# Waits by halves in a feed-forward phase; output moved into the next turn and a pipeline without work past its end in a recurrent phase

## The reference

```
ot = einsum('bhd,bhde->bhe', qt, S) + D * sum(qt * kt) * vt
kS = einsum('bhd,bhde->bhe', kt, S)
S  = at * (S - bt * kt[..., :, None] * kS[..., None, :]) + bt * kt[..., :, None] * vt[..., None, :]
```

## Time and profile before

| | |
|---|---|
| median of 3 runs | 4524.77 us |
| the profiled execution | 4536.98 us |
| its span, first to last instruction | 4535.2 us |
| PE busy | 4091.2 us (90%) |
| DVE busy | 3013.7 us (66%) |
| ACT busy | 1967.2 us (43%) |
| POOL busy | 1644.9 us (36%) |
| instructions | 93208 |

### The profile page before, as it was taken

The page is one execution under the profiler, slowest core; times in us unless marked ns, Lnnn a source line. Parts: engine busy times, 40 slices in busy tenths (PEclk is TensorE's granted clock), DMA queues, the critical chain, the costliest instruction groups (busy, mean ns, idle before and its releaser), DMA issues.

```text
span 4535.2 us, 93208 instructions
## 1 busy us (share of the span) xinstructions
PE 4091.2 (90%) x32914; PEld 2709.2 (60%) x32914; DVE 3013.7 (66%) x6409; ACT 1967.2 (43%) x4156; POOL 1644.9 (36%) x1479
## 2 busy tenths in 40 slices
PE   5999999999999999579999999989999999989998
PEld 4545555555555555347666767767676677667666
DVE  3555555555555555487777867867677678778677
ACT  2444444444444443244534435444445445444454
POOL 2111111111111111145454645555464556456454
PEclk9999999999999999798898998998998989989999
DMA  2000000000000000111111111111111111111111
GB/s 99 1 15 1 15 1 15 1 15 1 15 1 15 1 15 1 62 30 32 28 32 24 31 33 31 24 45 19 31 38 21 40 24 31 34 31 24 45 19 35
DMA packets 316505, 110.49 MB, mean 24 GB/s; under 512 B 290096, under 2 KB 303664, under 8 KB 315184
## 3 DMA queue, kind: packets, MB, share of 16 engines
q1 hardware_dynamic: 315968, 103.69, 9.7%
HBM read 77.45 MB, written 26.74 MB: 23 GB/s over the span
## 4 chain that ended last, share of the span: by engine, by line
PE 35%; DVE 11%; issue 5%; ACT 4%; POOL 1%; DMA 1%; SPq 1%; DVEq 0%; POOLq 0%; ACTq 0%
PE d_ps L1780 6%; DVE d_acc L1465 4%; PE d_ps L1856 3%; PE d_ps L1979 3%; PE d_ps L1964 3%; PE d_ps L1999 3%; PE d_ps L1818 2%; PE d_ps L1758 2%; PE d_ps L1893 1%; PE d_ps L1835 1%; PE d_ps L1907 1%; PE d_ps L1827 1%; DVE d_pw L1568 1%; PE d_ps L1797 1%; DVE d_AT L1514 1%
## 5 line engine op out<-in xcount | busy, mean ns | idle before, releaser
L229 POOL TENSOR_TENSOR f_qk<-f_m 128x512 f32<-128x512 f32 x128 | 162.8, 1272 | 1463.7 <-DVE f_m L412 1463.7
L1465 DVE SCALAR_TENSOR_TENSOR d_acc<-d_ps,d_cw,d_acc 128x511 f32<-128x511 f32 (+2 forms) x630 | 468.3, 744 | 81.8 <-ACT d_acc L1248 65.9
L1780 PE MATMUL d_ps<-d_xnT,d_wqkv 128*128 128x512 f32 x840 | 478.6, 700 | 0.2 <-DVE d_acc L1465 0.2
L312 ACT ACTIVATE f_pr<-f_sm,f_nb,f_qsc 128x256 f32<-128x256 f32 (+1 forms) x512 | 289.1, 566 | 160.9 <-DVE f_nb L440 159.1
L689 PE MATMUL f_ps<-f_m,f_w 128*128 128x512 f32 (+1 forms) x768 | 338.5, 595 | 22.6 <-DVE f_m L484 22.6
L1248 ACT ACTIVATE d_acc<-d_ps,d_cw 128x512 f32<-128x512 f32 x210 | 162.4, 774 | 396.6 <-PE d_ps L1780 394.7
L1126 POOL TENSOR_TENSOR d_rn<-d_ss,d_mhalf 128x8 f32<-128x8 f32 x137 | 236.5, 1726 | 253.2 <-DVE d_ss L1486 250.6
L434 DVE CUSTOM_DVE_ANT_0 f_sm<-f_ps,f_mask 128x256 f32<-128x256 f32 (+1 forms) x512 | 179.2, 387 | 210.4 <-PE f_ps L604 207.2
L1121 POOL TENSOR_TENSOR d_qk<-d_m 128x512 f32<-128x512 f32 x138 | 174.8, 1266 | 380.2 <-DVE d_m L1476 372.6
L1283 ACT ACTIVATE d_m<-d_qk 128x512 f32<-128x512 f32 x138 | 86.7, 628 | 421.3 <-POOL d_qk L1121 421.3
L689 PEld LDWEIGHTS f_ps<-f_m,f_w 128*128 128x128 f32 (+1 forms) x768 | 134.4, 178 | 222.9 <-issue 187.1
(11 more groups left out here) (210 smaller groups left out, 9694.0 us busy)
## 6 DMA issues: line engine op xcount, KB each, us to landing
d_wqkv<-in_dwqkv SPq DMA_DIRECT2D x36, 768.0 KB, 4.6
blocks_scratch<-d_LT SPq DMA_DIRECT2D x136, 64.0 KB, 2.0
d_T<-inverse_scratch SPq DMA_DIRECT2D x136, 64.0 KB, 2.2
f_xin<-in_x SPq DMA_DIRECT2D x9, 512.0 KB, 4.1
d_xnT<-xnT_scratch SPq DMA_DIRECT2D x9, 512.0 KB, 5.3
d_xnG<-xnT_scratch SPq DMA_DIRECT2D x9, 512.0 KB, 6.6
d_LB<-blocks_scratch SPq DMA_DIRECT2D x68, 64.0 KB, 2.8
inverse_scratch<-d_TB SPq DMA_DIRECT2D x68, 64.0 KB, 5.0
```

The lines of the kernel that those rows point to most:

```text
L312: nc.scalar.activation(pr[:, u % AHEAD, j, k0:], sm[:, u % AHEAD, j, k0:], ACT.Exp, bias=nb[:, u % AHEAD, j:j + 1], scale=qsc[:, 0, w, h:h ...
L1465: V.scalar_tensor_tensor(out=a[:, k:], in0=ps[:, CV_BANK[n], 0:T - k], scalar=cw[:, X, s * CT + t, TAPS - 1 - k:TAPS - k], in1=a[:, k:], o ...
L1780: last = mm(ps[:, CV_BANK[n], :], wqkv[:, X, k, t * P:(t + 1) * P], xnT[:, k, :], start=k == 0, stop=k == KC - 1)
```

## The change

The first phase: three of the eight copies of q/k transposes (`DVE_TURN = (3, 5, 7)`) go to DVE under a semaphore of their own; the output projection is made for the first three windows (384 tokens) ahead of the last window's transpose and copy, and then for the last 128 tokens; the q/k projections and the up projection wait for each half of their input where they use it.

The second phase: `group(b, k)` says which group a stage works on and returns nothing outside 0 to 31; each stage is left out where there is none. The prologue is the same code at steps -3 to 0, the loop runs 7 times over 4 steps, and the last three turns and the last output stand behind it. `output` of batch b is called in the tail of the first turn of batch b+1: product 0 behind convolution 0, product 1 behind convolution 1, transposes behind convolution 3, into banks 0 and 1. z is its own gate tile, the squares of the output heads go to the tile of the rotation (m12) and no more to oT. L1911 is gone: DVE transposes the 32-row blocks of Rf into T64.

```diff
+DVE_TURN = (3, 5, 7)
...
+                def copy_qkT(n):
+                    part, w = TURN[n]
+                    dve.wait_ge(qkT_ps, 1 + it * 2 * NT + n + 1)
+                    nc.vector.tensor_copy((qT, kT)[part][:, :, w * P:(w + 1) * P],
+                                          ps[:, 4 + n % 2, :].rearrange("p (a t) -> p a t", a=PAIRS)).then_inc(qkT_dve, 1)
+
                 sum_squares(2 * NT - 1)
                 inverse_norm(0)
+                copy_qkT(DVE_TURN[0])
...
+                for n in DVE_TURN[1:]:
+                    copy_qkT(n)
...
                     for c in range(KC):
+                        if n == 0 and l == 0:
+                            pe.wait_ge(xT_rdy, 1 + b * KC + c + 1)
+                        elif n == 0:
+                            pe.wait_ge(x2_rdy, 1 + it * KC - KC + c + 1)
...
+                split = (NT - 1) * P
+                pe.wait_ge(oT_rdy, 1 + it * NT + NT - 1)
+                pe.wait_ge(sm_rdy, 1 + it * NT * FH + NT * FH)
+                project_o(0, 0, split)
                 transpose_o(NT - 1)
+                project_o(1, 0, split)
                 pe.wait_ge(oT_rdy, 1 + it * NT + NT)
                 for c in range(KC):
+                    project_o(c, split, T).then_inc(wo_ps, 1)
...
-                pe.wait_ge(xc_rdy, 1 + it * KC + KC)
...
+                            if m == 0 and part == 0:
+                                pe.wait_ge(xc_rdy, 1 + it * KC + c + 1)
...
+    def group(b, k):
+
+        if isinstance(b, int) and not 0 <= b * NG + k < B * NG:
+            return None
+        return b * NG + k, k % NG, b + k // NG
...
         def merge32_end(i):
-            dve.wait_ge(t32_ps, 1 + i + 1)
-            V.tensor_scalar(T64[32:64, :, 0:32], ps[32:64, 0, :].rearrange("p (q t) -> p q t", q=NQ), -1.0, None,
-                            ALU.mult).then_inc(t64_rdy, 1)
+            dve.wait_ge(rf_b, 1 + 2 * i + 1)
+            V.transpose(T64[32:64, :, 0:32], Rf[0:32, :, 32:64]).then_inc(t64_rdy, 1)
...
+            if put is not None:
+                pe.wait_ge(xo_rdy, 1 + put * 2 + 2)
...
-            q2 = slice(32, 64)
-            for m in range(NQ):
-                last = mm(ps[q2, 0, 32 * m:32 * m + 32], R32[q2, m, :], Y32[q2, m, :], start=True, stop=True)
-            last.then_inc(t32_ps, 1)
...
+        for step in range(-3, 1):
+            turn(0, step)
+        with pe.Fori(0, B - 1) as b:
+            for step in range(1, NG + 1):
+                turn(b, step)
+        for step in range(1, NG):
+            turn(B - 1, step)
+        for m in range(KC):
+            output(B - 1, B * NG - 1, m)
+        output_T(B - 1)
```

More of the change, by code:

```diff
@@ L988, in hd, with late, done @@
         return ap.rearrange("p (h d) -> p h d", h=n)
-    def osq(s):
-        return oT[:, s * CT:(s + 1) * CT, :].rearrange("p a t -> p (a t)")
+    def group(b, k):
+        if isinstance(b, int) and not 0 <= b * NG + k < B * NG:
+            return None
+        return b * NG + k, k % NG, b + k // NG
+    def late(i, k):
+        return not isinstance(i, int) or i >= k
+    def done(now):
+        return now[2] - 1 if now and now[1] == 0 and late(now[2], 1) else None
     def val(i, n, k):
@@ new lines, in tail, with turn @@
+            if conv:
+                first_tap(i, s, 4)
+                squares(i, s, bt, 0)
+            if mid:
+                merge64(mid[0])
+            if conv:
+                silu(i, 4)
+                first_tap(i, s, 5)
+            if mid:
+                merge64_end(mid[0])
+            if conv:
+                silu(i, 5)
+                decay_exp(i, s, bt, 0)
+                squares(i, s, bt, 1)
+        def turn(b, step):
+            now, mid, made, conv = (group(b, step + k) for k in range(4))
+            tiles(made, now)
+            tail(conv, mid, now)
@@ L1419, in _ @@
+        act.wait_ge(init1, 1 + 5)
+        for step in range(-3, 1):
+            turn(0, step)
+        with act.Fori(0, B - 1) as b:
+            for step in range(1, NG + 1):
+                turn(b, step)
+        for step in range(1, NG):
+            turn(B - 1, step)
     @block.vector
@@ new lines, in tail @@
+            if conv:
+                i, s, bt = conv
+                conv_items(i, s, range(0, 1))
+            if done(now) is not None:
+                output(done(now), 0)
+            if gated is not None:
+                gates(gated)
+            if conv:
+                conv_items(i, s, range(1, 2))
+            if done(now) is not None:
+                output(done(now), 1)
+            if mid:
+                merge16_mid(mid[0])
+            if sub:
+                substitute(sub[0])
@@ new lines, in tail, with turn @@
+            if conv:
+                intake(i, s, bt, 0)
+                conv_items(i, s, range(4, 5))
+                norms(i, s, bt, 0)
+                intake(i, s, bt, 1)
+                conv_items(i, s, range(5, 6))
+        def turn(b, step):
+            now, mid, made, conv = (group(b, step + k) for k in range(4))
+            tiles(made, now)
+            tail(conv, made, mid, now)
+        dve.wait_ge(init1, 1 + 5)
+        for step in range(-3, 1):
+            turn(0, step)
+        with dve.Fori(0, B - 1) as b:
+            for step in range(1, NG + 1):
+                turn(b, step)
@@ L1728, in _ @@
+        for step in range(1, NG):
+            turn(B - 1, step)
+        for m in range(KC):
+            output(B - 1, m)
+        output_end(B - 1)
     @block.tensor
@@ L1790, in intake @@
                     pe.wait_ge(v_rdy, 1 + i * NT)
-            if c == 2 and s == 2 and not isinstance(i, int):
-                pe.wait_ge(xo_rdy, 1 + 2 * bt)
             if c != 1:
@@ L1810, in decay_sums @@
             n = lambda k=1, m=1: i * NT * m + c * m + k
-            if c == 0 and not isinstance(i, int):
+            if c == 0 and late(i, 3):
                 pe.wait_ge(oT_rdy, 1 + CT * (i - 2))
@@ L2010, in _, with tiles @@
         gate_sums(0)
-        def tiles(i, s, bt, now=None):
+        def tiles(made, now):
             for c in range(NT):
@@ new lines, in tail, with turn @@
+            if mid:
+                merge64(mid[0], mid[1] % 2)
+            if conv_g:
+                conv(*conv_g, 5)
+                decay_sums(*conv_g, 0)
+            if mid:
+                merge64_end(mid[0])
+        def turn(b, step):
+            now, mid, made, conv_g = (group(b, step + k) for k in range(4))
+            tiles(made, now)
+            tail(conv_g, mid, now)
+        pe.wait_ge(init1, 1 + 5)
+        for step in range(-3, 1):
+            turn(0, step)
+        with pe.Fori(0, B - 1) as b:
+            for step in range(1, NG + 1):
+                turn(b, step)
```

492 lines of the change are left out of this document (229 added, 263 removed).

## The result

The changed kernel takes **4366.17 us** (median of 4 runs, 4358.44 to 4370.99) against 4533.16 for the kernel before on the same chip (4 runs, 4518.47 to 4563.15): the ratio is 0.9627, 95% interval 0.9593 to 0.9661. The forecast was 4372, with a range of 4320 to 4430. The two profiled executions differ by 169.5 us of span (4535.2 and 4365.7), and the working goes by these.

What follows compares the result with a forecast made beforehand. The prediction took TensorE to bound the kernel. Savings of 50 + 30 + 23 + 50 = 153 us from 4537 gave 4384, and 12.2 less for the median gave 4372 us, range 4320 to 4430.

Steps and rivals of the forecast that it cites:

- the slow clock at the end: Half of a rival (chance 0.12, 4422 us): the drain runs cold, saving 23 us instead of 50.
- First phase, 50: First phase, all layers: shorter TensorE waits save 50 us in sum, with ends of 24 and 72.
- the split projection: First phase, attention output: projecting 384 of 512 columns ahead of the wait saves 1.28 us per layer.
- Around the up projection: First phase: the up projection starts on the first half of its input, saving 0.6 us per layer.
- the two edits there: First phase: new layer starts on its first half (0.84 or 0.9 us saved); copies 3, 5, 7 on VectorE (0.4).
- The stop before the first scores: First phase, behind the query/key copies: of this 0.78 us stop about 0.4 goes, possibly 0 or all.
- Block transpose, 30: Second phase: VectorE transposes the block instead of TensorE's matmuls, 1.1 us a turn, 30 us saved; ends 0 and 50.
- Output in the next turn, 23: Second phase: moving a batch's output into the next tail removes 19.1 us gaps, saving 23 us; ends -14 and 45.
- The loop's end: Second phase, in the moved output's sum: the loop end is still paid, 1.2 of 2.16 us.
- The rival that the product stalls VectorE: Other half of the rival with chance 0.12 (4422 us): TensorE and VectorE take turns, the moved output saves nothing.
- No work past the end, 50: End of the program: dropping work beyond the data saves 50 us, between 67 (warm) and 23 (all at 0.50 clock).
- Slower by a lower clock: Rival, chance 0.03: the lower clock takes the second phase, 8.8 us a turn, 264 in all, giving 4636 us.

Runs made afterwards that it cites:

- e_block_only: The kernel before with the new first phase and the block transpose, the output still in its own turn: 4423.65 us, ratio 0.977.
- e_matmul_block: The changed kernel with the 32-row block made by 32 matmuls and a scaling copy again: 4416.69 us, ratio 0.974.
- e_whole_projection: The changed kernel with the attention output projected whole again, after its last transpose: 4415.26 us, ratio 0.9743.

## Why the forecast was right, and where it was not

- *The whole*: 169.5 us of span against 153 summed. The forecast's case held, and of the rivals only the slow clock at the end showed in part. That the time itself came within 6 us is partly luck. The sum gives 4384 for a profiled execution and 4367.5 was measured; the 12.2 then taken off for the median hid most of that, as the changed kernel's profiled execution lies within 1.3 of its median. And the terms were off by +29.7, 0 and -13.2 us in the table above.
- *First phase, 50, measured 76* (and 4 more in the turns ahead of the first tail). This is the mis-sized term. It left out the clock. In the kernel before the granted clock falls 12 times in the first phase: in five of the projections (8.6 to 8.8 us), in four projections of q, k and v behind the stop of 1.55 and in three layers behind the stop of 0.78 before the scores. Each costs some 1.7 us, 20 in all, and in the changed kernel there is none. The rest, 56, is near the 50. By the rows of the two kernels the stretch with the split projection is 36.9 us shorter, of it 8 by the clock, against 20 forecast; taken out of the changed kernel it is worth 43, as the clock then falls in seven layers. Its stops are worth 1.8 a layer and not 1.28: besides 1.53 of waiting, a row that follows another without a stop starts some 0.15 us before that one's end. Around the up projection it is 9.6 (9.6 forecast), from one layer's end to the next one's first scores 23 (20 forecast for the two edits there, and 7 of the 23 are clock), and in the attention steps 5, all clock. These edits were not taken apart by runs. The stop before the first scores stayed at 0.78 us, now for VectorE's copy; by the trace the scores start 0.5 us earlier in the layer, since the stops before them got shorter.
- *Block transpose, 30*: 29 or 37 over 28 turns by e_block_only, depending on which of the two kernels with the old block it is read against, and 35 by e_matmul_block, with 11 more in the last three turns. The mechanism is as forecast. In turn 28 the excess is a lower clock behind small matmuls, which lies within the upper bound of 50 that was named for it; elsewhere it is within the scatter.
- *Output in the next turn, 23*: 19.5. Right in size, but by two errors. The loop's end was taken from VectorE's stop of 2.16, as 1.2 us of new stop, though TensorE's own in the same rows is 3.22. It costs 5.9 (7.45 less the 1.53 that the same place shows without a loop end), because the moved order puts 2.3 MB of transfers right ahead of it. So a turn with output that ends a loop takes 87.4 to 93.1 us, above the 84 to 86 forecast, and the one where no loop ends 80.3, below them. The rival that the product stalls VectorE did not come: L1966 does not wait, L1982 waits 1.10 where 0.5 was forecast.
- *No work past the end, 50*: 36.8. Both cases, 67 at the high clock and 23 at the low, were priced from the earlier trace rows; the value between was taken too near the high one. From tail 29 to the last projection it is 39 shorter, and the projection itself, 16.64 in place of 13.99, gives 2.6 back. The granted clock is 0.60 from tail 29 to the end, where it was 0.93. The wide products win some 14 back, less than 67 - 36, since a round with them is still 6.18 against the 5.3 that was estimated and the last of them end 7.4 us late.
- *Slower by a lower clock*: in turns 0 to 28 the granted clock is 0.91 in both kernels, so this did not come. In the first phase it rose; only at the end it fell, and that end is shorter all the same.

## What to carry to other kernels

A stop of TensorE costs its own length and, in some of its places, what the clock takes behind it: compare one operation's duration over all layers, and where it has two values, price the stop with the difference. A stretch in which small products wait for one another was helped here by wide products between them and not by transposes; put in no more of them than the wait holds. And put no large transfer right ahead of a loop's end.

## What was not expected of the hardware

- Stops of 0.84 and 0.69 us, with 0.66 us of work between them, were enough in 7 of 16 layers of e_whole_projection (5 of 16 before) for the projection behind them to take 8.8 and twice 10.1 in place of 7.13 us; with the stops filled this was gone.
- For 29 us TensorE was busy without a break, on small products and transposes, at a granted clock of 0.50 (1.2 GHz); with 512-column products among them the same 29 us had 0.97.
- The loop's end stopped TensorE for 7.45 us behind 2.3 MB of transfers and for 3.31 where none of them stood right ahead of it, as a 16 KB packet of the instruction queue started 4.2 us into the stop or at its begin; GpSimd's stops there shrank from 34.3 to 15.7 us in sum.
